# A two-layer graph network on one Trainium2 core: VectorE's instructions with two SBUF inputs cut into pieces of 128 columns

## The chip, the cores and the metric

The kernel runs on one NeuronCore of a Trainium2 chip, in a single launch. The metric is the device time of that launch in microseconds; the median of three runs counts. The engines are named as in the profile: PE is TensorE's matrix unit and PEld its weight loads, DVE is VectorE, ACT is ScalarE, POOL is GpSimd, SP is SyncE.

## The reference

There are 3,125 nodes of 128 features and 103,125 edges, sorted by destination, with 64 "radial" and 32 "spherical" features and one cutoff weight each. Cut to what matters:

```python
# layer 0: normalised graph convolution, residual, layer norm
norm = deg_inv_sqrt[src] * deg_inv_sqrt[dst]
h = x @ weight
out = segment_sum(norm[:, None] * h[src], dst)
x = layernorm(x + out + bias)
# layer 1: edge attention, residual, layer norm
w_ij = mlp(edge_64, rad_w0, rad_b0, rad_w1, rad_b1) + mlp(edge_32, sph_w0, sph_b0, sph_w1, sph_b1)  # hidden 256, silu
q, k, v = (x @ wq)[dst], (x @ wk)[src], (x @ wv)[src]          # 8 heads of 16
alpha = (q * w_ij * k).sum(per head) / sqrt(16) * cutoff
x = layernorm(x + segment_sum(alpha[..., None] * v, dst) / 16)
```

## The kernel before

Edges are padded to 202 groups of 512; a group is four tiles of 128 edges. An engine runs its own instruction list, and semaphores tie the lists together; the order on each engine is written out by hand.

**Sweep 1** (about 85 to 580 us of the span) has 51 unrolled steps. A step gathers seven tiles of source rows with indirect DMAs that POOL issues (line 794), sums them into a window of nodes by one-hot matmuls on PE (`sum1`, `add_tile`, line 1092), counts the rest of the edges with small one-hot products (lines 1475, 1476, 1492 on DVE), and runs the edge MLP for every fourth group, whose product goes to DRAM through `w_sb`. This product is the "stored" one.

**Sweep 2** (about 604 to 1665 us) has 51 steps of four groups: three unrolled, a loop of 11 turns with four steps in each, and four unrolled. For each group POOL gathers key and value rows eight groups ahead (`gather`, line 784, four indirect DMAs a group). PE expands the queries (`expand_q`, line 1218) and sums messages into the node window (`sum2`, line 1092). Of the four groups of a step, `g`, `g + 1`, `g + 2` and `g + 3`, the first takes its MLP product from DRAM through `w_sb` in SBUF; the other three have it computed on PE (`layer1`, lines 1066 and 1068; `layer2`, line 1084) and read it from PSUM.

On DVE a group passes through `times_k` (line 1670: key rows times queries), `times_w` (line 1682: times the MLP product), `head_sums` (line 1687), `times_cutoff` (line 1700) and `message` (line 1708: value rows times the attention factor). The factor of the stored group lies in `alpha` in SBUF, that of the others in PSUM. Around these stand `one_hot_t` (line 1661, the one-hot for `expand_q`), `one_hot` (line 1447, the one-hot for the sums), `add_pair` (line 1468) and `split_lo` (line 1454). MLP inputs are split into a rounded high half by ACT (line 892) and a low half by `split_lo`, 64 partitions by 1,024 columns in four instructions of 256; `layer1` reads both. One `split_lo` runs per sweep-1 step and three per sweep-2 step.

The order on DVE at the end of one step of sweep 2 and the head of the next is `one_hot_t(g + 6)`, `one_hot`, `times_k(g + 4)`, and then, with `g` now the next step's, `times_w(g - 1)`, `times_w(g)` from `w_sb`, `head_sums(g - 1)`, `split_lo`, `times_cutoff(g - 1)`, `times_k(g + 1)`, `message(g - 1)`, `head_sums(g)`, `one_hot_t(g + 3)`, `times_cutoff(g)`, `message(g)`. `one_hot_t(g + 6)` waits for PE's `expand_q(g + 4)`. On PE the list between those two points is the second half of one step and the first MLP group of the next:

```python
                expand_q(first + 4)
                expand_q(first + 5)
                sum2(first + 2)
...
                mlp_group(mlps[0], first + 1)
                expand_q(first + 2)
                if not s.before(1):
                    sum2(first - 1)
```

`sum2(first - 1)` waits for `message(g - 1)`.

Of the kernel before, what the change touches and what calls it, by code (L numbers as in the profile page):

```python
# [19 lines left out]
P = 128  # L20
WIN = 42
PARTS = 3
DIGITS = 64
TILES = 4
GE = P * TILES
HEADS, HD = 8, 16
RAD, SPH, HID = 64, 32, 256
# [18 lines left out]
F32 = mybir.dt.float32  # L46
# [3 lines left out]
ALU = mybir.AluOpType  # L50
# [83 lines left out]
def ds(start, size):  # L134
    return bass.DynSlice(start, size)


def build(nc, x, x_pad, src_idx, src_e, dst_e, dst_row, dst_first, cut_e, rad_t, sph_t, w_l0, b_l0, rad_w0, rad_b0,
          rad_w1, rad_b1, sph_w0, sph_b0, sph_w1, sph_b1, wq, wk, wv, out):
    N, D = x.shape  # L140
# [27 lines left out]
    with ExitStack() as ctx:  # L168
        def sb(name, shape, dt=F32):
            return ctx.enter_context(nc.sbuf_tensor(name, shape, dt))  # L170
# [6 lines left out]
        def sem(name):  # L177
            return ctx.enter_context(nc.semaphore(name))
# [21 lines left out]
        onehot = sb("onehot", [P, 2, 2 * TILES + 2, WIN])  # L200
        qwin = sb("qwin", [P, 2, D], BF16)
        xraw = sb("xraw", [RAD, 3, 2, GE])
        xsplit = sb("xsplit", [P, 2, 2, GE], F32R)
        hid = sb("hid", [P, 2, 4, GE])
        w_sb = sb("w_sb", [P, 2, TILES * D])
# [7 lines left out]
        rel = sb("rel", [P, COLS])  # L213
# [22 lines left out]
        iota_win = sb("iota_win", [P, WIN])  # L236
# [27 lines left out]
        def part(tile, at, n):  # L264

            return tile[:, at:at + n], at + n
# [7 lines left out]
        prod, to = part(late, 0, 2 * TILES * D)  # L274
        prod = prod.rearrange("p (k f) -> p k f", k=2)
        msg, to = part(late, to, 2 * TILES * D)
        msg = msg.rearrange("p (k t f) -> p k t f", k=2, t=TILES)
# [49 lines left out]
        w1_ps, w2_ps = bank[4:5], bank[3:5]  # L327
# [73 lines left out]
        mlp1, mlp2 = MlpSemaphores(sem, sems, 1, 2), MlpSemaphores(sem, sems, 2, 3)  # L401
# [6 lines left out]
        s_qkw = sem("s_qkw")  # L408
        s_red = sem("s_red")
        s_al = sem("s_al")  # L410
        s_msg = sem("s_msg")
# [874 lines left out]
        def _(dve):  # L1286
# [60 lines left out]
            for j in range(2):  # L1347
                own = slice(XS_DVE[j], XS_DVE[j + 1])
# [54 lines left out]
            for b in range(0, NB, 2):  # L1403
                own = slice(b, min(NB, b + 2))
                last = dve.tensor_tensor(xs_lo[:, own, :], xs_sb[:, own, :], xs_hi[:, own, :].bitcast(F32), ALU.subtract)
# [36 lines left out]
                dve.wait_ge(s_pass2, p * PASS2 + PASS2)  # L1442

            def one_hot(s, first=2 * TILES, n=2 * TILES):
                at = rel[:, ds(s.n * first, n)].unsqueeze(2).to_broadcast([P, n, WIN])
                nodes_in = iota_win[:, :].unsqueeze(1).to_broadcast([P, n, WIN])
                return dve.tensor_tensor(onehot[:, s.slot(2), 0:n, :], at, nodes_in, ALU.is_equal)

            def split_lo(s, mlp):
                dve.wait_ge(mlp.s_hi, s.tick + 1)  # L1450
                k, b = s.slot(mlp.ring), s.slot(2)
                for m in range(2):
                    for half in (slice(0, GE // 2), slice(GE // 2, GE)):
                        last = dve.tensor_tensor(xsplit[RAD:P, b, m, half], xraw[:, k, m, half],  # L1454
                                                 xsplit[0:RAD, b, m, half].bitcast(F32), ALU.subtract)
                last.then_inc(mlp.s_lo, 1)

            def load(row, first, n, most):
# [36 lines left out]
            def sweep1(s):  # L1495
                own = batches(s)
                if s.before(1):
                    one_hot(s, GATHERED, tiles1(s)).then_inc(s_hot1, 1)
                    split_lo(s, mlp1)
                    split_lo(s + 1, mlp1)  # L1500
                    for j in range(HOTS):
                        hots(own[0] + j)
# [15 lines left out]
                if product(s):  # L1518
                    span_bases = load(span_i, (product(s) * SPANS).n, SPANS, NP - 1)
                    if own:  # L1520
                        more_hots(own[0])
                        if not s.is_last(2):
                            split_lo(s + 2, mlp1)
                        dve.wait_ge(s_sum1, s.tick)
                        one_hot(s + 1, GATHERED, tiles1(s + 1)).then_inc(s_hot1, 1)
                    dve.wait_ge(s_acc1, s.tick)
                    add_spans(product(s), span_bases)
                    if own:
                        add_counts(own[0], offsets[0])
                        next_offset()  # L1530
                    batch(1)
                else:
                    batch(0)
                    batch(1)
                    if not s.is_last(2):
                        split_lo(s + 2, mlp1)
                batch(2)
                if not product(s):
                    if not s.before(1):
                        dve.wait_ge(s_sum1, s.tick)  # L1540
                    one_hot(s + 1, GATHERED, tiles1(s + 1)).then_inc(s_hot1, 1)
# [110 lines left out]
            def kv(g):  # L1652
                return gath2[:, g.slot(RING2), :].rearrange("p (t c f) -> p t c f", t=TILES, c=2)
# [19 lines left out]
            def times_w(g, s=None, m=None):  # L1673
                j = g.slot(2)
                dve.wait_ge(s_qk, g.tick + 1)
                if m is None:
                    dve.wait_ge(s_wload[s.slot(2)], (s.round(2) + 1) * 16)
                    w = w_sb[:, s.slot(2), :]
                else:
                    dve.wait_ge(mlp2.s_w, m.tick + 1)  # L1680
                    w = w2_ps[m.slot(2)][:, :]
                dve.tensor_tensor(prod[:, j, :], prod[:, j, :], w, ALU.mult).then_inc(s_qkw, 1)  # L1682

            def head_sums(g, turn=None):
                j = g.slot(2)
# [4 lines left out]
            def factors(m):  # L1690

                if m is None:
                    return alpha[:, :, :]
                return w2_ps[m.slot(2)][:, 0:TILES * HEADS].rearrange("p (t h) -> p t h", t=TILES)
# [7 lines left out]
            def message(g, m=None, turn=None):  # L1702
                j = g.slot(2)
                a = factors(m).unsqueeze(3).to_broadcast([P, TILES, HEADS, HD])
                dve.wait_ge(s_al, (turn or g).tick + 1)
                if not g.before(2):
                    dve.wait_ge(s_sum2, (g - 2).tick + 1)
                dve.tensor_tensor(msg[:, j, :, :].rearrange("p t (h d) -> p t h d", d=HD),  # L1708
                                  kv(g)[:, :, 1, :].rearrange("p t (h d) -> p t h d", d=HD), a,
                                  ALU.mult).then_inc(s_msg, 1)  # L1710
# [6 lines left out]
            def last_step2(s):  # L1717
                g, m, pairs = s.sub(4, 0, G), mlps2(s), pairs2(s)
                bases = load(base_i, s.n * 2 - 1, 2, NP - 1)
                times_w(g, s=s)  # L1720
                head_sums(g, turn=g - 1)
                times_cutoff(g, turn=g - 1)
                message(g, turn=g - 1)
                dve.wait_ge(s_relrow, s.p * 16 + 16)
                next_rows()
                times_w(g - 1, m=m[0] - 1)
                head_sums(g - 1, turn=g)
                times_cutoff(g - 1, m[0] - 1, turn=g)
                message(g - 1, m[0] - 1, turn=g)
                times_k(g + 1)  # L1730
                times_w(g + 1, m=m[0])
                head_sums(g + 1)
                times_cutoff(g + 1, m[0])
                message(g + 1, m[0])
                add_pair(pairs[0] - 1, bases[0])
                add_pair(pairs[0], bases[1])
# [81 lines left out]
class PRE:  # L1818
# [6 lines left out]
    half = 21  # L1825
# [3 lines left out]
class SET:  # L1829

    rel = 5
# [65 lines left out]
```

## Time and profile before

| | |
|---|---|
| time, median of 3 runs | 1691.49 us (1691.41 to 1692.15) |
| the profiled execution's own time | 1685.36 us |
| its span | 1683.5 us |
| PE busy | 1535.1 us (91%) |
| DVE busy | 1356.2 us (81%), 3810 instructions |
| POOL busy | 1215.7 us (72%) |
| ACT busy | 955.0 us (57%) |
| mean granted PE clock | 0.98 of full speed |

Busy time is the union of an engine's instructions. A row of the timeline gives start, length, line and shape; two DVE instructions can overlap, so the distance from one start to the next is what an instruction holds up its successor, and the length is what its reader waits for.

### The profile page before, as it was taken

The numbers are of one execution on the slowest core, as the hardware profiler recorded it, in microseconds if no ns is written. First come the engines' busy times: TensorE is split into PE (matmuls) and PEld (weight loads), VectorE is DVE, ScalarE is ACT, GpSimd is POOL, SyncE is SP. The second block draws the span as 40 slices with busy tenths as digits, with TensorE's granted clock in tenths as the row PEclk, the third lists the DMA queues.
The fourth block names the chain that finished last, engine by engine and source line by source line (L and its number), as shares of the span: only waits on it lengthen the run. The fifth ranks groups of instructions, "written<-read, shape, count | busy, mean of one in ns | idle before, by whom it ended". The sixth has DMA issues, their size and how long they took to land.

```text
span 1683.5 us, 43509 instructions
## 1 busy us (share of the span) xinstructions
PE 1535.1 (91%) x12636; PEld 1426.1 (85%) x12636; DVE 1356.2 (81%) x3810; ACT 955.0 (57%) x1410; POOL 1215.7 (72%) x1201
## 2 busy tenths in 40 slices
PE   4379999999999759999999999999999999999995
PEld 3267988888898749998989898989898989898995
DVE  9988779797887457887888787888787878887886
ACT  3344646566565465665656565655555656565664
POOL 5677777777777247777777777777777777777772
PEclk9999999999999889999999999999999999999998
DMA  4133334343433286666666666666666666666673
GB/s 123 39 97 108 109 102 116 108 121 103 116 108 97 64 231 170 189 190 172 186 183 184 174 186 173 185 182 180 180 180 180 184 178 185 181 186 179 183 190 115
DMA packets 176755, 257.32 MB, mean 153 GB/s; under 512 B 80278, under 2 KB 91213, under 8 KB 176476
## 3 DMA queue, kind: packets, MB, share of 16 engines
q0 software_dynamic: 50240, 129.44, 29.1%
q1 hardware_dynamic: 123100, 124.61, 25.0%
q10 hardware_dynamic: 3264, 1.64, 0.3%
q8 instruction: 48, 0.79, 0.2%
q14 instruction: 103, 0.84, 0.2%
HBM read 232.76 MB, written 22.79 MB: 152 GB/s over the span
## 4 chain that ended last, share of the span: by engine, by line
PE 66%; POOL 13%; issue 8%; DVE 7%; DMA 3%; ACT 1%; DVEq 1%; SPq 1%; POOLq 0%; ACTq 0%
PE bank L1084 33%; POOL arena L794 13%; PE bank L1092 12%; PE bank L1066 9%; PE bank L1068 4%; PE bank L1122 3%; PE bank L1218 3%; DVE arena L1323 2%; DMA arena<-xs_d,idx 1%; DMA idx<-in_src_e 1%; PE bank L1114 1%; DVE xsplit L1454 1%; DVE late L1670 1%; ACT nodes L948 0%; DVE red L1687 0%
## 5 line engine op out<-in xcount | busy, mean ns | idle before, releaser
L784 POOL DMA_INDIRECT arena<-kv_d,idx x808 | 802.5, 993 | 273.2 <-issue 259.8
L1084 PEld LDWEIGHTS bank<-w,hid 128*128 128x128 f32 x6464 | 781.9, 192 | 27.2 <-issue 1.9
L1084 PE MATMUL bank<-w,hid 128*128 128x128 f32 x6464 | 790.9, 276 | 0.0
L900 ACT ACTIVATE hid<-bank,b 128x512 f32<-128x512 f32 x808 | 500.6, 683 | 273.1 <-PE bank L1068 260.2
L794 POOL DMA_INDIRECT arena<-xs_d,idx x358 | 354.6, 991 | 128.8 <-issue 124.5
L1066 PE MATMUL bank<-xsplit,w_hi 128*128 128x512 f32 x808 | 347.7, 441 | 26.3 <-DVE xsplit L1454 26.3
L1454 DVE TENSOR_TENSOR xsplit<-xraw,xsplit 64x256 fp32r<-64x256 f32 x808 | 288.0, 414 | 7.3 <-ACT xsplit L892 1.0
L1092 PE MATMUL bank<-onehot,late 128*128 128x126 f32 x1616 | 219.2, 285 | 33.6 <-DVE late L1708 31.7
L1092 PEld LDWEIGHTS bank<-onehot,late 128*128 128x128 f32 x1616 | 196.7, 195 | 36.9 <-DVE late L1708 33.6
L892 ACT ACTIVATE xsplit<-xraw 64x1024 fp32r<-64x1024 f32 x202 | 210.7, 1044 | 2.6 <-DMA xraw<-in_sph_t 1.7
L884 ACT ACTIVATE bank<-b_full 128x512 f32<-128x512 f32 x199 | 119.3, 599 | 160.4 <-DVE late L1708 158.8
L1066 PEld LDWEIGHTS bank<-xsplit,w_hi 128*128 128x128 f32 x808 | 157.5, 195 | 50.1 <-DVE xsplit L1454 24.5
L1661 DVE TENSOR_SCALAR late<-late,iota_part 126x512 bf16<-126x512 bf16 x202 | 71.0, 352 | 115.5 <-PE bank L1218 113.9
L1068 PE MATMUL bank<-xsplit,w_lo 128*128 128x512 f32 x404 | 163.8, 405 | 0.0
L1492 DVE TENSOR_TENSOR count<-count,bank 128x300 f32 x225 | 103.9, 462 | 59.9 <-PE bank L1114 46.4
L1670 DVE TENSOR_TENSOR late<-arena,bank 128x512 f32<-128x512 f32 x202 | 137.8, 682 | 7.0 <-PE bank L1218 5.4
L1682 DVE TENSOR_TENSOR late<-late,bank 128x512 f32<-128x512 f32 x151 | 103.0, 682 | 47.8 <-issue 32.7
L1476 DVE TENSOR_SCALAR key_hot<-iota_key,key 128x300 bf16<-128x300 bf16 x450 | 140.9, 315 | 0.0
L1687 DVE TENSOR_REDUCE red<-late 128x32 f32<-128x512 f32 x202 | 137.1, 679 | 0.1
L919 ACT ACTIVATE w_sb<-bank 128x512 f32<-128x512 f32 x51 | 30.5, 598 | 163.3 <-PE bank L1084 163.3
L1475 DVE TENSOR_SCALAR low_hot<-iota_key,low_f 128x128 bf16<-128x128 bf16 x450 | 117.7, 262 | 3.2 <-issue 3.1
L1092 PE MATMUL bank<-onehot,arena 128*128 128x126 f32 x716 | 93.2, 278 | 17.3 <-DMA arena<-xs_d,idx 17.1
(159 smaller groups left out, 1358.6 us busy)
## 6 DMA issues: line engine op xcount, KB each, us to landing
xraw<-in_rad_t SPq DMA_DIRECT2D x207, 128.0 KB
xraw<-in_sph_t SPq DMA_DIRECT2D x414, 64.0 KB
late<-relrow_d SPq DMA_DIRECT2D x103, 256.0 KB, 3.9
w_sb<-w_d SPq DMA_DIRECT2D x52, 256.0 KB
w_d<-w_sb SPq DMA_DIRECT2D x51, 256.0 KB
arena<-kv_d,idx POOLq DMA_INDIRECT x808
arena<-xs_d,idx POOLq DMA_INDIRECT x358
qwin<-q_d SPq DMA_DIRECT2D x101, 31.5 KB
```

The lines of the kernel that those rows point to most:

```text
L784: pool.indirect_dma_start(gath[:, k, t * width:(t + 1) * width], None, table, bass.IndirectOffsetOnAxis(ap=idx[:, pair.slot(4), j * TILES ...
L794: pool.indirect_dma_start(gath1[s.slot(RING1)][:, t * D:(t + 1) * D], None, xs_d, bass.IndirectOffsetOnAxis(ap=idx[:, s.slot(4), t:t + 1], ...
L892: act.activation(xsplit[0:RAD, s.slot(2), :, :], xraw[:, k, :, :], ACT.Copy).then_inc(mlp.s_hi, 1)
L900: act.activation(hid[:, s.slot(2), c, :], hid_ps[s.sub(4, c, 4 * s.total).slot(len(hid_ps))][:, :], ACT.Silu, bias=b0[:, c:c + 1]).then_in ...
L1066: mm = pe.matmul(to, w0_hi[:, m, cols], xsplit[:, b, m, :], start=True, stop=(m == 1))
L1068: mm = pe.matmul(to, w0_lo[:, m, cols], xsplit[:, b, m, :], start=False, stop=True)
L1084: mm = pe.matmul(w_ps[:, t * D:(t + 1) * D], hid[:, b, c, t * P:(t + 1) * P], w1[:, c, :], start=False, stop=(c == 3), skip_group_check=True)
L1092: return pe.matmul(bank[7][:, 0:3 * WIN], rows, onehot[:, b, k:k + 3, :].rearrange("p t n -> p (t n)"), start=(k == 0), stop=(k == n - 1), ...
L1454: last = dve.tensor_tensor(xsplit[RAD:P, b, m, half], xraw[:, k, m, half], xsplit[0:RAD, b, m, half].bitcast(F32), ALU.subtract)
L1476: last = dve.tensor_scalar(key_hot[:, at_tile + t, :], iota_key[:, :], key[:, ds(col, 1)], None, ALU.is_equal)
L1670: dve.tensor_tensor(prod[:, j, :].rearrange("p (t f) -> p t f", t=TILES), kv(g)[:, :, 0, :], q_ps[j][:, :].rearrange("p (t f) -> p t f", t ...
L1687: dve.tensor_reduce(red[:, j, :, :].rearrange("p t h -> p (t h)"), prod[:, j, :].rearrange("p (h d) -> p h d", d=HD), AX.X, ALU.add).then_ ...
```

## The change

Four kinds of DVE instruction are cut along their columns; the data, the order and the waits stay, and the semaphore is raised by the last piece. `split_lo` has eight instructions of 128 columns for four of 256. `times_w` and `message` of the stored group have four of 128 for one of 512. `one_hot` has two of at most four tiles (168 columns each, or 168 and 126) for one.

```diff
             def one_hot(s, first=2 * TILES, n=2 * TILES):
-                at = rel[:, ds(s.n * first, n)].unsqueeze(2).to_broadcast([P, n, WIN])
-                nodes_in = iota_win[:, :].unsqueeze(1).to_broadcast([P, n, WIN])
-                return dve.tensor_tensor(onehot[:, s.slot(2), 0:n, :], at, nodes_in, ALU.is_equal)
+                for t in range(0, n, TILES):
+                    k = min(TILES, n - t)
+                    at = rel[:, ds(s.n * first + t, k)].unsqueeze(2).to_broadcast([P, k, WIN])
+                    nodes_in = iota_win[:, :].unsqueeze(1).to_broadcast([P, k, WIN])
+                    last = dve.tensor_tensor(onehot[:, s.slot(2), t:t + k, :], at, nodes_in, ALU.is_equal)
+                return last
...
                 for m in range(2):
-                    for half in (slice(0, GE // 2), slice(GE // 2, GE)):
-                        last = dve.tensor_tensor(xsplit[RAD:P, b, m, half], xraw[:, k, m, half],
-                                                 xsplit[0:RAD, b, m, half].bitcast(F32), ALU.subtract)
+                    for t in range(TILES):
+                        own = slice(t * P, (t + 1) * P)
+                        last = dve.tensor_tensor(xsplit[RAD:P, b, m, own], xraw[:, k, m, own],
+                                                 xsplit[0:RAD, b, m, own].bitcast(F32), ALU.subtract)
...
                 if m is None:
                     dve.wait_ge(s_wload[s.slot(2)], (s.round(2) + 1) * 16)
-                    w = w_sb[:, s.slot(2), :]
-                else:
-                    dve.wait_ge(mlp2.s_w, m.tick + 1)
-                    w = w2_ps[m.slot(2)][:, :]
-                dve.tensor_tensor(prod[:, j, :], prod[:, j, :], w, ALU.mult).then_inc(s_qkw, 1)
+                    for t in range(TILES):
+                        own = slice(t * D, (t + 1) * D)
+                        last = dve.tensor_tensor(prod[:, j, own], prod[:, j, own], w_sb[:, s.slot(2), own], ALU.mult)
+                    last.then_inc(s_qkw, 1)
+                    return
+                dve.wait_ge(mlp2.s_w, m.tick + 1)
+                dve.tensor_tensor(prod[:, j, :], prod[:, j, :], w2_ps[m.slot(2)][:, :], ALU.mult).then_inc(s_qkw, 1)
...
+                if m is None:
+                    for t in range(TILES):
+                        last = dve.tensor_tensor(msg[:, j, t, :].rearrange("p (h d) -> p h d", d=HD),
+                                                 kv(g)[:, t, 1, :].rearrange("p (h d) -> p h d", d=HD), a[:, t, :, :], ALU.mult)
+                    last.then_inc(s_msg, 1)
+                    return
```

## Rows read from the trace of the kernel before

**Rows 1.** Busy time by stretch: stretch, length, engines, granted clock, DMA share, GB/s.

```profile
900.00:1100.00 200.00, 193.13 (x1561) 184.08 (x1560) 164.95 (x389) 117.74 (x175) 153.33 (x154) 0.97 0.66 180
```

**Rows 2.** PE's waits, whole run: who waited for whom, us in total, times, longest.

```profile
PE bank L1092 <- DVE late L1708: 31.7, 11, 3.7
PE bank L1066 <- DVE xsplit L1454: 26.3, 3, 14.8
PE bank L1092 <- DMA arena<-xs_d,idx: 17.1, 16, 1.8
```

**Rows 3.** DVE's waits from 700 to 1500 us, a stretch of sweep 2.

```profile
DVE late L1661 <- PE bank L1218: 90.1, 39, 2.4
DVE late L1682 <- issue: 29.2, 9, 3.9
```

**Rows 4.** PE's timeline: start, length, instructions; in brackets the idle time before.

```profile
307.61 0.93 PE L1092 MATMUL bank<-onehot,arena 128*128 128x126 f32 x6 [1.15 <-DMA arena<-xs_d,idx]
...
861.65 1.16 PE L1092 MATMUL bank<-onehot,late 128*128 128x126 f32 x8 [2.86 <-DVE late L1708]
...
1028.29 2.08 PE L1092 MATMUL bank<-onehot,late 128*128 128x126 f32 x8 [3.57 <-DVE late L1708]
...
1081.91 0.61 PE L1218 MATMUL bank<-qwin,late 126*128 126x128 bf16 x8
...
1088.27 0.39 PE L1218 MATMUL bank<-qwin,late 126*128 126x128 bf16 x4
1088.49 1.11 PE L1092 MATMUL bank<-onehot,late 128*128 128x126 f32 x8
```

**Rows 5.** DVE's timeline, at a loop turn and in three later steps of sweep 2.

```profile
1027.55 0.68 DVE L1708 TENSOR_TENSOR late<-arena,bank 128x512 f32<-128x512 f32 x1
...
1057.84 0.20 DVE L1700 TENSOR_TENSOR bank<-red,cut 128x32 f32<-128x32 f32 x1
1057.94 0.35 DVE L1661 TENSOR_SCALAR late<-late,iota_part 126x512 bf16<-126x512 bf16 x1
...
1064.69 0.69 DVE L1682 TENSOR_TENSOR late<-late,w_sb 128x512 f32<-128x512 f32 x1
...
1082.33 0.35 DVE L1661 TENSOR_SCALAR late<-late,iota_part 126x512 bf16<-126x512 bf16 x1 [2.30 <-PE bank L1218]
1082.60 0.50 DVE L1447 TENSOR_TENSOR onehot<-rel,iota_win 128x336 f32<-128x336 f32 x1
1083.02 0.68 DVE L1670 TENSOR_TENSOR late<-arena,bank 128x512 f32<-128x512 f32 x1
1083.62 0.68 DVE L1682 TENSOR_TENSOR late<-late,bank 128x512 f32<-128x512 f32 x1
...
1085.53 1.43 DVE L1454 TENSOR_TENSOR xsplit<-xraw,xsplit 64x256 fp32r<-64x256 f32 x4
...
1087.70 0.68 DVE L1708 TENSOR_TENSOR late<-arena,bank 128x512 f32<-128x512 f32 x1
```

**Rows 6.** `split_lo` as a group by line and shape: busy us, mean ns, idle before.

```profile
L1454 DVE TENSOR_TENSOR xsplit<-xraw,xsplit 64x256 fp32r<-64x256 f32 x808 | 288.0, 414 | 7.3 <-ACT xsplit L892 1.0
```

**Rows 7.** Line 1670, `times_k`, whole run: its lengths, then its only idle time before.

```profile
L1670 DVE TENSOR_TENSOR late<-arena,bank x202: 677/681/689, 624.8 to 1660.0; 128x512 f32<-128x512 f32 x101
...
  PE bank L1218: 5.4, 1
```

**Rows 8.** POOL's timeline in sweep 2, three gathers in a row.

```profile
1064.89 1.31 POOL L784 DMA_INDIRECT arena<-kv_d,idx  x1 [0.30 <-issue]
1066.51 1.08 POOL L784 DMA_INDIRECT arena<-kv_d,idx  x1 [0.31 <-issue]
1067.89 0.94 POOL L784 DMA_INDIRECT arena<-kv_d,idx  x1 [0.30 <-issue]
```

**Rows 9.** The gathers as groups by line: busy us, mean ns, idle before.

```profile
L784 POOL DMA_INDIRECT arena<-kv_d,idx x808 | 802.5, 993 | 273.2 <-issue 259.8 <-DVE late L1708 13.4
...
L794 POOL DMA_INDIRECT arena<-xs_d,idx x358 | 354.6, 991 | 128.8 <-issue 124.5 <-DMA idx<-in_src_e 3.7 <-PE bank L1092 0.6
```

## The prediction

> **What bounds the kernel now.** I read the busy times by stretch first. In sweep 2 PE is busy for 193.13 of 200 us, DVE for 164.95 [rows 1]: PE sets the pace there, and DVE looks as if it had room. A mean cannot say where that room lies, so I went on to the waits. From 700 to 1500 us DVE waits 39 times, 2.3 us each, before `one_hot_t(g + 6)` for PE's `expand_q`, once in each step [rows 3]. PE itself waits for `message` before `sum2` 11 times in the run, 31.7 us together [rows 2]. Ten of these follow a stall of DVE's own, about 3 us of "issue" when its loop jumps back [rows 3].
>
> The timelines of one ordinary step then show how much room there is. PE starts its pair of `expand_q` at 1081.91; DVE, waiting for it, starts `one_hot_t` at 1082.33 [rows 4, 5]. From there DVE runs without a pause through `one_hot`, `times_k`, both `times_w`, `head_sums`, `split_lo`, `times_cutoff`, `times_k` to `message(g - 1)`, which ends at 1087.70 + 0.68 = 1088.38. PE wants it at 1088.49, right behind the `expand_q` that began at 1088.27 [rows 4, 5]. At the turn, where PE does stand waiting, it starts 0.06 us after the message ends (1027.55 + 0.68 = 1028.23, then 1028.29). So the ordinary step has a cover of 0.11 - 0.06 = 0.05 us. DVE's 2.3 idle microseconds stand ahead of this chain, which PE itself starts; they cannot be spent inside it. That is the place to price the change: whatever lengthens the stretch from `one_hot_t` to `message(g - 1)` by more than 0.05 us lengthens the step, because PE is full for the rest of it.
>
> **What a piece costs.** An instruction holds up the next by the distance between starts: 0.10 us for 32 columns (1057.84 to 1057.94), 0.60 for 512 (1083.02 to 1083.62) [rows 5]; for 256 it is (1.43 - 0.414) / 3 = 0.339 [rows 5, 6]. The line from 32 to 256 columns has 1.067 ns a column and 0.066 us fixed. A piece of 128 columns thus holds 0.203, one of 168 0.245.
>
> - `split_lo`: 8 x 0.203 for 4 x 0.339: 1.62 for 1.36, +0.26.
> - `times_w` of the stored group: 4 x 0.203 for 0.60: +0.21. `message` of the stored group: the same.
> - `one_hot`: 2 x 0.245 for 0.42 (1082.60 to 1083.02 [rows 5]): +0.07.
>
> The lower bound for eight more instructions in the chain is nothing, if pieces overlapped wholly, but even 32 columns hold 0.10. The line through 256 and 512 columns gives 0.078 fixed and 0.62 for the chain. The upper bound is that pieces don't overlap at all: a length of 0.414 - 128 x 0.001067 = 0.277 each gives 2.22 for 1.36, 1.11 for 0.60 and, with 0.50 - 0.18 = 0.32, 0.64 for 0.42, or +1.6 us. I take 0.066, since the pieces are of the kind that the 1.43 us row already shows overlapping.
>
> By the Trainium skill ("VectorE: DVE Perf Modes", section "The DRAIN you can't avoid") the next instruction cannot issue until the pipe is empty, and instruction count is what to keep down. By that the sum would be near the upper bound; the rows, four of 0.414 in 1.43, do not show so long a gap.
>
> **The chain, step by step.** It holds one `one_hot`, the stored `times_w` and one `split_lo`: 0.07 + 0.21 + 0.26 = +0.54 us. `message` of the stored group and the other two `split_lo` come behind `message(g - 1)`; they take 0.21 + 0.07 + 2 x 0.26 = 0.8 us from DVE's wait. That wait goes from 2.3 to 2.3 + 0.5 (PE is later by so much) - 0.54 - 0.8, or about 1.4 us, so it still covers them. If that cover went, the whole 1.4 us a step would show.
>
> Of 51 steps 49 have this `sum2` (the first has no earlier group, the last is written apart). Ten follow a jump back of the loop and wait already: 10 x 0.54 = 5.4. The other 39 have 0.05 of cover: 39 x 0.49 = 19.1. Together +24.5 us.
>
> **The clock at the turns.** After an idle 3.57 us eight matmuls took 2.08 us, after 2.86 us 1.16, after none 1.11 [rows 4]. A longer idle at the turns can put some of the undisturbed ones on the lower level; two more at about 1 to 1.5 us are +2.5, between 0 and 8. The 0.5 us idle of an ordinary step should not do it: six matmuls behind 1.15 us of idle took 0.93 [rows 4].
>
> **Ends.** Each pass begins with a `split_lo` for which PE stands waiting [rows 2], and DVE's last step has a stored `message` on its path: about +1.
>
> **Sweep 1 and POOL.** Here something can be won. Line 794's gathers take 0.991 us in the mean [rows 9], while an undisturbed gather takes 0.94 [rows 8]. The long ones fall on the edited instructions: the gather at 1064.89 took 1.31 and began while `times_w` from `w_sb` ran (1064.69 to 1065.38) [rows 5, 8]. So a gather waits for the end of a DVE instruction with two SBUF inputs, and shorter pieces let it in sooner. In sweep 1 this lengthening is 358 x 0.05 = 18 us at most; `split_lo` and `one_hot` are only part of it, and halving them leaves some 5. PE waits 17.1 us there for gathers [rows 2], so it can use that; but `split_lo` and `one_hot` add 0.33 us to each of 51 steps on DVE. From -10 (more of the lengthening goes) to +17 (all of DVE's addition shows); I take -3, because PE waits for gathers in this sweep and not for DVE.
>
> **Sum.** 24.5 + 2.5 + 1 - 3 = +25 us against the profiled execution's 1685.36 (span 1683.5 and 1.9 around it): 1710. The median of the runs lies 6.1 us above that execution, which gives 1716.
>
> **Rivals.**
>
> *Gathers set the pace, and it gets faster.* POOL issues gathers through all of sweep 2 with 0.3 us between them [rows 8], 808 of 0.993 us [rows 9]. If their landing ended last, the change would give back about half of 808 x 0.05 = 40 us of lengthening, and 5 in sweep 1: -25, or 1666. It decides only from the point where `times_k` waits for a gather. Against it: no `times_k` waited for one; its only wait in the run is 5.4 us, once, for PE [rows 7]. Chance 0.07.
>
> The Trainium skill ("SBUF — State Buffer", section "SBUF: two separate sides") has the rule behind this: a port pair shared by VectorE and GpSimd is locked for the whole instruction, also by one with two SBUF inputs. The long gathers agree; what that does for the time hangs on who waits for them.
>
> *DVE's room hides it, and nothing changes.* 1.4 us more a step fit into 2.3 of idle; with -3 and +1 the time would be 1690. For it stands the mean load [rows 1], against it the order: 0.05 us of cover in the chain. Chance 0.07.
>
> *Pieces cost their whole length, or the clock falls in ordinary steps.* +1.6 in the chain would be 49 x 1.55 = 76 us, 1767; half of that, or some 20 to 30 steps with a falling clock at 1 us, 1735 to 1745. Against it are the overlapping four of `split_lo` and the 1.15 us idle above. Chance 0.08.
>
> **How the numbers follow.** The forecast has 0.78, with 1703 to 1732 as its own range: 0.62 instead of 0.54 in the chain (+4), the clock (-2.5 to +5.5), sweep 1 (-7 to +20, both ends unlikely). The range 1698 to 1732 leaves out the faster rival, nearly all of the one that hides it and most of the dear one, together just under 0.2. A change of 0.2% (3.4 us) is about what measurement here can tell from none. Faster has the first rival's 0.07, same the second's 0.07, slower 0.86.
>
> **What would show it.** Right: in the changed kernel's timeline PE is idle about half a microsecond before `sum2` in every ordinary step, ended by `message`; the waits' view has some 50 of these for 11 before, some 55 us together; DVE's wait before `one_hot_t` is near 1.4 us; eight `split_lo` pieces take about 1.7 us from first start to last end; gathers are shorter in the mean, near 0.97; an ordinary step of sweep 2 is half a microsecond longer. Wrong: DVE's wait is unchanged and PE's waits stay at 11 (the cover held), `times_k` waits for DMA (gathers paced it), pieces 0.28 us apart, or sweep 1 longer by 10 us.

## The result and the profile after

The changed kernel takes 1715.24 us in the median of 4 runs (1714.82 to 1715.6); the kernel before takes 1691.45 (1690.0 to 1692.15). The ratio is 1.0142, 95% interval 1.0126 to 1.0158: slower by 1.4%, 0.8 us from the forecast of 1716. The profiled execution took 1715.35 us, its span 1713.5.

Busy time from 900 to 1100 us, against [rows 1]:

```profile
900.00:1100.00 200.00, 189.74 (x1533) 179.54 (x1532) 175.62 (x568) 113.66 (x170) 145.77 (x152) 0.98 0.62 178
```

DVE has 568 instructions for 389 and is busy 10.7 us more; PE, which set the pace, is busy 3.4 us less. PE's waits in the whole run, against [rows 2]:

```profile
PE bank L1092 <- DVE late L1720: 50.8, 50, 3.9
...
PE bank L1066 <- DVE xsplit L1458: 27.0, 3, 15.2
PE bank L1092 <- DMA arena<-xs_d,idx: 13.1, 13, 1.9
```

Fifty waits for `message` (line 1720 now) where there were 11. DVE's waits from 700 to 1500 us, against [rows 3]:

```profile
DVE late L1665 <- PE bank L1218: 51.4, 37, 1.9
DVE late L1688 <- issue: 29.5, 9, 3.4
```

Before `one_hot_t` DVE waits 1.39 us for 2.31; the stall of "issue" at the jump back is as long as it was. The timelines of an ordinary step and of a turn, PE first, against [rows 4, 5]:

```profile
1097.52 0.39 PE L1218 MATMUL bank<-qwin,late 126*128 126x128 bf16 x4
1098.23 1.16 PE L1092 MATMUL bank<-onehot,late 128*128 128x126 f32 x8 [0.32 <-DVE late L1720]
...
1117.59 0.39 PE L1218 MATMUL bank<-qwin,late 126*128 126x128 bf16 x4
1121.63 1.57 PE L1092 MATMUL bank<-onehot,late 128*128 128x126 f32 x8 [3.65 <-DVE late L1720]
```

```profile
1091.59 0.35 DVE L1665 TENSOR_SCALAR late<-late,iota_part 126x512 bf16<-126x512 bf16 x1 [1.25 <-PE bank L1218]
1091.86 0.57 DVE L1449 TENSOR_TENSOR onehot<-rel,iota_win 128x168 f32<-128x168 f32 x2
...
1093.54 0.89 DVE L1684 TENSOR_TENSOR late<-late,w_sb 128x128 f32<-128x128 f32 x4
...
1095.05 1.70 DVE L1458 TENSOR_TENSOR xsplit<-xraw,xsplit 64x128 fp32r<-64x128 f32 x8
...
1097.50 0.68 DVE L1720 TENSOR_TENSOR late<-arena,bank 128x512 f32<-128x512 f32 x1
...
1116.33 0.69 DVE L1688 TENSOR_TENSOR late<-late,bank 128x512 f32<-128x512 f32 x1 [3.23 <-issue]
```

`message` ends at 1097.50 + 0.68 = 1098.18 and PE starts 0.05 us later. From the start of the last `expand_q` to `sum2` it is 0.71 us; in the step of [rows 4] it was 0.22 (1088.27 to 1088.49). So this step has 0.49 us more. Over the 39 ordinary steps that distance went from 0.25 to 0.72 us in the mean, and an ordinary step of the loop, from one such `sum2` to the next, from 19.59 to 20.08 us. (The bracket has only 0.32, since the `expand_q`'s own end is modelled later than its successor could have started.) The gathers, against [rows 9], came down:

```profile
L784 POOL DMA_INDIRECT arena<-kv_d,idx x808 | 779.7, 965 | 311.4 <-issue 262.8 <-DVE late L1720 48.6
L794 POOL DMA_INDIRECT arena<-xs_d,idx x358 | 350.7, 980 | 128.8 <-issue 126.4 <-DMA idx<-in_src_e 1.5 <-PE bank L1092 0.9
```

**Where the time went.** The two profiled executions differ by 30.0 us. The first gather of sweep 2 starts 1.3 us earlier (604.47 to 603.17), and from there to the first `sum2` that waits for `message(g - 1)` it is 0.2 us more; from that `sum2` to the 49th of its kind, one a step, it is 1013.86 us for 984.45 (+29.4); behind that +1.7. The +29.4 splits by steps. At each of ten turns, the step of the stall and the one after it take 45.17 us for 43.58, +1.59: 15.9. The other 28 steps have 0.48 each: 13.5.

### The profile page after: what moved, and what is told of

It reads as the page before. It is cut to its first block, busy times and chain, and to the rows that moved or that the text cites. A ratio compares the mean times of both kernels' runs of the same rounds, so it can differ in the third digit from the quotient of the medians.

```text
span 1713.5 us, 44863 instructions
## 1 busy us (share of the span) xinstructions
PE 1549.1 (90%) x12636; PEld 1433.0 (84%) x12636; DVE 1453.2 (85%) x5076; ACT 954.9 (56%) x1410; POOL 1190.2 (69%) x1201
## 4 chain that ended last, share of the span: by engine, by line
PE 49%; DVE 19%; POOL 14%; issue 11%; DVEq 3%; DMA 2%; ACT 1%; SPq 0%; POOLq 0%; ACTq 0%
PE bank L1084 24%; POOL arena L794 14%; PE bank L1092 10%; PE bank L1066 6%; DVE xsplit L1458 4%; PE bank L1068 3%; DVE late L1684 3%; DVE late L1674 2%; DVE arena L1323 2%; PE bank L1122 2%; DVE late L1720 2%; DVE red L1693 2%; DVEq L1464 1%; PE bank L1218 1%; PE bank L1114 1%
## 5 line engine op out<-in xcount | busy, mean ns | idle before, releaser
L784 POOL DMA_INDIRECT arena<-kv_d,idx x808 | 779.7, 965 | 311.4 <-issue 262.8
L794 POOL DMA_INDIRECT arena<-xs_d,idx x358 | 350.7, 980 | 128.8 <-issue 126.4
L1066 PE MATMUL bank<-xsplit,w_hi 128*128 128x512 f32 x808 | 351.9, 446 | 27.0 <-DVE xsplit L1458 27.0
L1458 DVE TENSOR_TENSOR xsplit<-xraw,xsplit 64x128 fp32r<-64x128 f32 x1616 | 346.3, 280 | 6.4
L1066 PEld LDWEIGHTS bank<-xsplit,w_hi 128*128 128x128 f32 x808 | 159.4, 197 | 51.5 <-DVE xsplit L1458 24.9
L1665 DVE TENSOR_SCALAR late<-late,iota_part 126x512 bf16<-126x512 bf16 x202 | 77.1, 382 | 70.8 <-PE bank L1218 66.3
L1092 PE MATMUL bank<-onehot,arena 128*128 128x126 f32 x716 | 92.2, 277 | 13.3 <-DMA arena<-xs_d,idx 13.1
```

Of the source, the lines that this page charges most:

```text
L784: pool.indirect_dma_start(gath[:, k, t * width:(t + 1) * width], None, table, bass.IndirectOffsetOnAxis(ap=idx[:, pair.slot(4), j * TILES ...
L794: pool.indirect_dma_start(gath1[s.slot(RING1)][:, t * D:(t + 1) * D], None, xs_d, bass.IndirectOffsetOnAxis(ap=idx[:, s.slot(4), t:t + 1], ...
L1066: mm = pe.matmul(to, w0_hi[:, m, cols], xsplit[:, b, m, :], start=True, stop=(m == 1))
L1092: return pe.matmul(bank[7][:, 0:3 * WIN], rows, onehot[:, b, k:k + 3, :].rearrange("p t n -> p (t n)"), start=(k == 0), stop=(k == n - 1), ...
L1458: last = dve.tensor_tensor(xsplit[RAD:P, b, m, own], xraw[:, k, m, own], xsplit[0:RAD, b, m, own].bitcast(F32), ALU.subtract)
```

## The experiments

Theory A is the prediction's reason: the cuts on the chain from `one_hot_t` to `message(g - 1)` cost 0.49 us a step, those behind it are covered. Its first rival now is that the other cuts, or the gathers, carry the difference. Line numbers of the experiments are up to a dozen off from those above.

**Only the chain's cuts** (against the kernel before, with the stored `times_w` in four as in the change):

```diff
-                split_lo(m[2], mlp2)
+                split_lo(m[2], mlp2, 128)
...
-                one_hot(pairs[1] + 1)
+                one_hot(pairs[1] + 1, cut_up=True)
```

> Only the three instructions of sweep 2 that stand in the chain from one_hot_t(g + 6) to message(g - 1) are cut: the stored times_w, the split_lo before times_cutoff, the one_hot ahead of times_k(g + 4). All else is as before. Theory A (the chain has 0.05 us of cover, so what is in it shows and what is behind it does not): nearly the whole loss, 1713 to 1719, PE idle about 0.49 us before sum2 in each ordinary step. Theory B (VectorE's added load shows, wherever it stands): 0.54 of 1.35 us per step, so some 10 us, 1701. Theory C (shorter pieces matter through GpSimd's gathers): GpSimd's mean gather in sweep 2 falls by what the times_w and a third of the split_lo collisions cost, and the time falls below 1690.

Measured: 1750.44 us (1749.19 to 1754.61), ratio 1.0372 [1.0352, 1.0392]. The ordinary step is 20.07 us (one in four 20.37), with the 0.49 us before `sum2` that theory A wants, but the total is 35 us too long. DVE's timeline at a turn shows why:

```profile
1043.17 0.69 DVE L1690 TENSOR_TENSOR late<-late,bank 128x512 f32<-128x512 f32 x1 [3.82 <-issue]
1046.17 0.90 DVE L1686 TENSOR_TENSOR late<-late,w_sb 128x128 f32<-128x128 f32 x4 [2.32 <-issue]
```

At each turn there are two stalls of "issue", 3.8 and 2.0 us in the mean of ten, where the kernel before and the changed kernel have one. Nothing in the second instruction's inputs is late: its load from DRAM was issued 25 us ahead of it (1020.59), and loads of this kind land in some 4 us. This was not in any theory.

**Only the cuts behind the chain** (stored `message` in four, the other two `split_lo` in eight, the other one-hot in two; cut to the lines on `split_lo`, against the kernel just above):

```diff
-                size = size or (256 if mlp is mlp1 else 256)
+                size = size or (256 if mlp is mlp1 else 128)
...
-                split_lo(m[2], mlp2, 128)
+                split_lo(m[2], mlp2, 256)
```

> The opposite half of sweep 2: only the stored message, the two split_lo behind message(g - 1) and the one_hot behind it are cut, 0.8 us more VectorE time per step. Theory A: PE's waits stay at about 11 and the time within 3 us of before, 1688 to 1695; VectorE's wait before one_hot_t falls from 2.3 to about 1.5 us. Theory B: 0.8 of 1.35 us per step, so some 14 us, 1705. Theory C: below 1690.

Measured: 1672.77 us (1669.3 to 1674.08), ratio 0.9905 [0.9888, 0.9922]: faster than both kernels, and by its time alone theory C's. The ordinary step is 19.6 us at first, so these cuts are covered (from the 18th step on steps are longer, for the reason found in the next section). But the stalls at the turns are gone, and with them half of the traffic of the queue that loads instructions (packets, MB, share), the kernel before first:

```profile
q14 instruction: 103, 0.84, 0.2%
```

```profile
q14 instruction: 54, 0.44, 0.1%
```

So the turn's stall looks like a wait for instructions, whose absence may have won the time in theory C's place. The Trainium skill ("Runtime: NRT & Kernel Launch", section "Instruction fetch mechanics") says that an engine holds two blocks of 256 instructions, and that a taken branch whose target is in neither forces a fetch. The fall of that queue's packets with the stalls agrees. I call it theory P: the stall hangs on where the loop of sweep 2 lies, and each experiment moves it.

**Only sweep 1's cuts** (cut to two of the lines, against the kernel just above):

```diff
-                size = size or (256 if mlp is mlp1 else 128)
+                size = size or (128 if mlp is mlp1 else 256)
...
-                    one_hot(s, GATHERED, tiles1(s), False).then_inc(s_hot1, 1)
+                    one_hot(s, GATHERED, tiles1(s), True).then_inc(s_hot1, 1)
```

> Only sweep 1's split_lo and one_hot are cut. Prediction's term: -3 us, from GpSimd being let in sooner (bounds -10 and +17). From the two traces I expect -1 to -3 us: 1688 to 1691, with the mean gather of line 794 at about 0.980 us for 0.991 and PE's waits for these gathers at about 13 us for 17. If VectorE's addition of 0.33 us a step shows instead: up to 1708.

Measured: 1689.29 us (1681.96 to 1693.49), ratio 0.9991 [0.9972, 1.001], between a gain of 4.7 us and a loss of 1.7. Line 794's gathers went from 991 to 978 ns.

**All cuts, the message of the group before moved ahead of `split_lo` and the stored `times_w`** (against the changed kernel):

```diff
-                times_w(g, s=s)
                 if not s.before(1):
                     head_sums(g - 1)
-                split_lo(m[2], mlp2)
-                if not s.before(1):
                     times_cutoff(g - 1, m[0] - 1)
-                times_k(g + 1)
-                if not s.before(1):
                     message(g - 1, m[0] - 1)
+                split_lo(m[2], mlp2, 128)
+                times_w(g, s=s)
+                times_k(g + 1)
```

> All cuts of the change stay, but in sweep 2 head_sums, times_cutoff and message of group g - 1 come right behind its times_w, ahead of split_lo, the stored times_w and times_k(g + 1). VectorE has the same work in another order. Theory A: the chain to message(g - 1) loses about 3.0 us of other work and gains some 0.3 us of latency between dependent instructions, so PE waits for no message in ordinary steps and about 1 us instead of 4 at the ten turns of the loop: 24 us of the change's loss and another 20 to 35 us at the turns come back, 1655 to 1672. Theory B: the same load, so 1715 or somewhat more for the latencies.

Measured: 1686.46 us (1683.93 to 1690.25), ratio 0.9989 [0.9976, 1.0001]. Most of the loss is gone, but 1655 to 1672 is missed. PE's waits:

```profile
PE bank L1066 <- DVE xsplit L1460: 40.8, 27, 15.2
...
PE bank L1092 <- DVE late L1722: 14.3, 19, 1.6
```

The ordinary step is back to 19.6 us with nothing ahead of `sum2`; near the turns `split_lo`, now behind the message, is late in its place, and DVE's stall there is unchanged (29.9 us in nine from 700 to 1500).

### Moving the loop

The next kernels have one-element memsets put ahead of sweep 2's loop, in idle time of DVE, which changes nothing in the loop but its place:

```diff
+                    if s.is_last(1):
+                        for k in range(39):
+                            dve.memset(unused[0:1, k:k + 1], 0.0)
                     dve.wait_ge(s_acc1, s.tick)
                     add_spans(product(s), span_bases)
```

**The kernel before, moved by 39.**

> The kernel before with 39 one-element memsets of VectorE put into its idle time at the end of sweep 1, so that the loop of sweep 2 stands 39 instructions later; the work of the loop is untouched. Theory P (the 3.3 us in which VectorE waits for nothing the profile shows, once at each of 9 to 10 turns of the loop, come from where the loop's instructions stand, not from what they do): these waits fall from 29 us to under 3. Then either the whole turn is won back (two steps of 43.6 us at a turn against 39.1 for two ordinary ones, 10 times: 1645 to 1650 us), or GpSimd's gathers, issued without a pause from 604 to 1652 us in the kernel before, become the bound and the time is 1678 to 1688 us; I take the second. Theory W (the waits belong to the turn itself): waits as before, 1689 to 1693 us.

Measured: 1680.41 us (1678.0 to 1685.25), ratio 0.9941 [0.9918, 0.9964]. No stall is left at any turn, and the instruction queue has 53 packets: theory P holds, theory W falls. Of the 32.7 us of stalls 11 came back, between the medians. The profiled execution is the slowest of the eight (1685.25 us), so its rows show what took the rest at its largest. PE now waits elsewhere, for `hid` 31 times in the run:

```profile
PE bank L1067 <- ACT hid L901: 27.8, 31, 1.7
...
PE bank L1093 <- DVE late L1720: 3.6, 11, 0.4
```

Steps are 19.55 us for the first thirteen (20.1 at the turns), then 19.8 to 21.8. In the POOL timeline 64 gathers (four steps) start 82.3 to 83.6 us apart here and 82.6 to 83.8 in the kernel before, whose turns are 82.9 us apart: there PE with its stall and the gathers kept the same pace by chance. Without the stall PE runs ahead until a group's last gather ends only 4 to 7 us before its `times_k` (11 to 18 in the loop of the kernel before), and from there the gathers are the bound. How they hold PE back is in two waits from 1300 to 1500 us, of SP's queue and of ACT, and in the chain of waits of that stretch:

```profile
SPq L522 <- DMA arena<-kv_d,idx: 83.5, 19, 5.2
```

```profile
ACT xsplit L893 <- DMA xraw<-in_sph_t: 23.1, 18, 2.6
```

```profile
by line: POOL arena L785 75.8%; issue 22.3%; POOLq L805 1.7%; POOLq L783 0.3%; POOLq L801 0.3%; POOLq L122 0.1%
```

Line 522 is SP's `load_idx`: it may reuse an index buffer only when the gathers that read it have landed. Behind it in SP's queue stand the loads of `xraw`; these come late, ACT's `split_hi` waits for them, `hid` is late, and PE with it. `times_k` waits for a gather once in the run, for 0.4 us.

**The chain's cuts alone, moved by 107.**

> The chain's cuts alone, as in the first experiment, with 107 memsets that move the loop so that its start is not at the end of a block of 256 instructions. Theory A (the chain from one_hot_t to the message costs 0.5 us a step, and the 35 us that the first experiment showed beyond the changed kernel came from a second wait for instructions at each turn): only one wait of about 3.3 us at a turn, ordinary step 20.05 us, 1712 to 1720 us, as the changed kernel. Rival (the chain's cuts really cost 60 us alone, and the other cuts give 35 back): 1745 to 1755 us again.

Measured: 1720.46 us (1718.41 to 1721.49), ratio 1.017 [1.0133, 1.0206]. One stall at a turn, ordinary step 20.08 us. PE's waits for `message` in the whole run, and DVE's stalls from 700 to 1500 us:

```profile
PE bank L1093 <- DVE late L1720: 52.4, 50, 4.2
```

```profile
DVE late L1694 <- issue: 31.4, 9, 3.8
```

There are fifty waits for `message`, as in the changed kernel: the chain's cuts alone make the loss of the whole change. Of the 30 us that the first experiment took above this, 29 lie in the pairs of steps at its ten turns. The second stall itself is 20 of them; the rest, with a longer first stall (3.8 us for 3.5), was not taken apart.

**The cuts behind the chain, moved by 76.**

> The cuts behind the chain alone (stored message, the two other split_lo, the other one-hot), as in the second experiment, with 76 memsets that move the loop to where one wait at each turn is to be expected again. Theory A (these cuts are covered by VectorE's idle time, and the 19 us won in the second experiment were the turn's wait): waits of 3 us at each turn are back, ordinary step 19.55 us, 1687 to 1694 us. Rival (the cuts themselves win time by keeping GpSimd's gathers short): 1670 to 1676 us again.

Measured: 1692.21 us (1687.17 to 1695.31), ratio 0.9998 [0.9979, 1.0017]. The stalls are back (31.4 us in ten), the ordinary step is 19.55 us. PE's waits for `message` in the whole run, and DVE's waits from 700 to 1500 us:

```profile
PE bank L1093 <- DVE late L1726: 30.8, 11, 3.3
```

```profile
DVE late L1671 <- PE bank L1219: 54.2, 37, 2.2
DVE late L1694 <- issue: 28.2, 9, 3.4
```

PE waits 11 times, as in the kernel before, and DVE's wait before `one_hot_t` falls to 1.46 us: it is what covers them. These cuts cost nothing that can be measured (-3.6 to +2.9 us), and the 19 us won in the second experiment were the stall's.

**The stored weight product in eight pieces of 64** (all other cuts as in the change):

```diff
-                    for t in range(TILES):
-                        own = slice(t * D, (t + 1) * D)
+                    for t in range(0, GE, 64):
+                        own = slice(t, t + 64)
```

> The changed kernel with the stored weight product in eight pieces of 64 columns instead of four of 128; its loop turns with one wait, as the changed kernel's. Theory A (each piece costs its fixed 0.066 us, all of it on the chain): four more pieces are 0.26 us a step, the wait of TensorE before sum2 grows from 0.49 to 0.75 us, 49 steps: 1715 + 13, that is 1726 to 1731 us. Rival (a shorter piece costs its full length anew, as the third rival of the prediction had it): step longer by over 0.5 us, 1740 us or more. Rival (slack is left): 1715 to 1718 us.

Measured: 1736.0 us (1733.14 to 1737.31), ratio 1.026 [1.0223, 1.0297]. DVE's eight pieces, and PE's last `expand_q` and `sum2`, in one step:

```profile
1062.59 1.17 DVE L1686 TENSOR_TENSOR late<-late,w_sb 128x64 f32<-128x64 f32 x8
...
1066.57 0.39 PE L1218 MATMUL bank<-qwin,late 126*128 126x128 bf16 x4
1067.56 1.16 PE L1092 MATMUL bank<-onehot,late 128*128 128x126 f32 x8 [0.60 <-DVE late L1722]
```

From start to start it is 0.99 us, 0.77 over the 0.22: four more pieces cost 0.28 us, 0.07 each, against 0.066 expected. The total is 5 us above the range: one step in four has 0.2 us more, which I did not follow up, and at all ten turns PE's eight matmuls took 1.79 to 2.08 us, for 1.37 to 1.68 in the changed kernel.

**The changed kernel with the chain's `split_lo` in four, moved by 28.**

```diff
-                split_lo(m[2], mlp2, 128)
+                split_lo(m[2], mlp2, 256)
```

> The changed kernel, but the split_lo on the chain in four instructions as before, with 28 memsets that keep the end of the loop where it stands in the changed kernel. Theory A (each instruction of the chain costs its fixed 0.066 us, TensorE's wait before sum2 is their sum less 0.05): four fewer are 0.26 us, the wait falls from 0.49 to 0.23 us, 49 steps: 1715 - 13, that is 1700 to 1705 us. Rival (split_lo is covered by its neighbours, the stored product alone holds the message back): 1713 to 1717 us.

Measured: 1706.3 us (1705.88 to 1709.8), ratio 1.0094 [1.0058, 1.013], 1 us above the range. Its step:

```profile
1090.20 0.39 PE L1219 MATMUL bank<-qwin,late 126*128 126x128 bf16 x4
1090.64 1.16 PE L1093 MATMUL bank<-onehot,late 128*128 128x126 f32 x8
```

0.44 - 0.22 = 0.22 us, where theory A says 0.23; ordinary step 19.80 us. So `split_lo` is 0.27 of the 0.49, the stored product and the one-hot the rest. The two steps of a turn take 45.09 us, nearly the 45.17 of the changed kernel although the chain is shorter by 0.54 in them: at seven of the ten the eight matmuls took 2.07 us, against 1.68 at most in the changed kernel. That accounts for the 4 us by which the gain of 13 fell short: 10 x (0.54 - 0.08) = 4.6.

**The changed kernel, moved by 225.**

> The changed kernel with 225 memsets ahead of sweep 2's loop (130 in the idle time at the end of sweep 1, 95 before the nodes' product), which put the start of the loop just behind the start of a block of 256 instructions and its end in the first half of the next but one. Theory P: no wait of VectorE for instructions at the turns, no fall of the clock there, ordinary steps of 20.07 us throughout, since the gathers are 14 us or more ahead; 10 turns of 45.2 us become 40.1: 1715 - 50, that is 1662 to 1672 us. The chain's cuts still cost their 0.49 us a step. Rival (GpSimd binds first, as in the kernel before moved): steps grow beyond 20.07 us and the time is 1675 to 1685 us. Rival W (no effect of the place): 1712 to 1718 us.

Measured: 1716.21 us (1713.06 to 1716.89), ratio 1.014 [1.0104, 1.0177]. The stalls stayed (33.7 us in ten), and so did the time, in rival W's range. Since 39 instructions did remove them from the kernel before, the place does count, but theory P as I had it was incomplete: a loop that starts behind a block's start can still be too long.

**The early message with all cuts, moved by 225.**

> All cuts, the message of the group before moved ahead of split_lo, the weight product and times_k (as in the fourth experiment), and the loop moved by 225 memsets as in the run beside it. If the fourth experiment missed its 1655 to 1672 us through the waits at the turns, they are gone here: ordinary step 19.6 us at first, then GpSimd's gathers bind, at a mean of 0.963 us against 0.99 in the kernel before moved (808 of them, 22 us less than its 1680): 1655 to 1668 us. Rival (the early message makes split_lo late in every step): ordinary step over 20 us, 1670 us or more.

Measured: 1688.13 us (1683.58 to 1693.67), ratio 0.9981 [0.9965, 0.9998]. The stalls stayed here too (36.1 us in ten), the time is that of the fourth experiment, and the 1655 to 1668 are missed with it.

**The early message, all `split_lo` and the stored `times_w` cut, one-hots and stored message whole, moved by 34** (cut to two of the lines, against the kernel above):

```diff
-                one_hot(pairs[1] + 1, cut_up=True)
+                one_hot(pairs[1] + 1, cut_up=False)
...
-                        for k in range(130):
+                        for k in range(34):
```

> All three split_lo and the stored weight product cut, the one-hots and the stored message whole, the message of the group before moved ahead of the chain (as in the fourth experiment), and 34 memsets; the loop is 329 instructions long, starts just behind the start of a block of 256 and ends 76 into the next but one, two instructions short of where the second experiment's loop ended, which had no wait at its turns (the changed kernel moved, 30 further on, had it at each). Theory: no wait at the turns; the cuts are off the path of sum2, so ordinary steps are 19.55 us; gathers of sweep 2 at a mean of 0.965 to 0.972 us against 0.990 in the kernel before moved (808 of them, 15 to 20 us off its 1680), so 1658 to 1668 us. Rival (the loop is too long and waits at each turn after all): 1682 to 1690 us, as the two runs with the early message. Rival (gathers stay at 0.98 us and bind): 1669 to 1676 us.

Measured: 1672.12 us (1668.6 to 1678.09), ratio 0.989 [0.9865, 0.9916], by the second rival's range. There is no stall at any turn, and the first steps take 19.55 us with nothing before `sum2`, although `split_lo` and `times_w` are cut: the same pieces off the chain are free. From the 18th step on the gathers bind again, in the same way (from 1300 to 1500 us SP's `load_idx` waits 85.5 us for them), at a mean of 0.980 us:

```profile
L785 POOL DMA_INDIRECT arena<-kv_d,idx x808 | 791.5, 980 | 271.9 <-issue 267.7 <-DVE late L1720 4.3
```

With the second experiment it is the fastest here, 1.1% below the kernel before and 2.5% below the changed one.

### What the places say together

Places are counted from the program's order, modulo the 256 instructions that a block has by the Trainium skill ("Runtime: NRT & Kernel Launch", section "Instruction fetch mechanics"), plus 24. The 24 is an estimate: it puts the block's end between the two instructions of the first experiment that stall one after the other. All these loops reach into a second block; the first experiment's reaches into a third.

| kernel | instructions in loop | starts at | ends at | stalls at a turn |
|---|---|---|---|---|
| before, moved by 39 | 269 | 8 | 20 | none |
| early message, moved by 34 | 329 | 4 | 76 | none |
| cuts behind the chain | 321 | 14 | 78 | none |
| changed, moved by 225 | 357 | 6 | 106 | one, 3.4 us |
| changed | 357 | 37 | 137 | one, 3.3 us |
| chain moved by 107 | 305 | 100 | 148 | one, 3.5 us |
| before | 269 | 225 | 237 | one, 3.3 us |
| chain only | 305 | 249 | 41 | two, 3.8 and 2.0 us |

No stall is seen when the loop starts just behind a block's start and ends within 78 instructions of the next. The kernels left out here stall once at each turn and fit: sweep 1's cuts alone lie at 224 to 236, the eight pieces at 49 to 165, `split_lo` in four at 53 to 137, the cuts behind the chain moved by 76 at 90 to 154, and the two with all cuts and the early message where the changed kernel and the changed one moved by 225 lie. (The expectations of the kernels moved by 225 and by 34 put the end into the next block but one; by this count it is the next.) Why an end at 106 is too far when the start lies in the block just before it, the runs don't show.

## Why the prediction was right, and where it was mis-sized

- **The chain** was right in kind and size. Predicted: 0.54 us in DVE's chain, 0.05 of cover, 24.5 us. Measured: 0.48 in the ordinary step and, at each of ten turns, 1.11 in two steps (from the last `expand_q` to `sum2` 4.13 and 0.74 us, for 3.53 and 0.23, in the mean): 28 x 0.48 + 10 x 1.11 = 24.5 us. The cover was read from one step; it is the usual one, but in the kernel before every fourth step had none, with 0.30 to 0.33 us from the last `expand_q` to `sum2` where the others have 0.22. The chain alone makes the loss (moved by 107: 1720.46), the rest alone none (moved by 76: 1692.21), four instructions less take 0.27, four more add 0.28, and moved off the path to `sum2` they cost nothing.
- **The price of a piece** was right: eight `split_lo` in 1.70 us, four of `times_w` in 0.89; by the forecast's figures 7 x 0.203 + 0.277 = 1.70 and 3 x 0.203 + 0.277 = 0.89. The rival that pieces cost their whole length falls with the dose: 0.07 us for one more. The section of the Trainium skill weighed there ("VectorE: DVE Perf Modes", "The DRAIN you can't avoid") has the next operation wait until the pipe is empty, but also says that one which is not held starts earlier; the forecast weighed only the first. The pieces did start earlier: one of 64 columns held up the next by (1.17 - 0.219) / 7 = 0.14 us, at a mean length of 0.219.
- **The clock at the turns** was the term that was mis-sized: +2.5 was forecast between the profiled executions; what is left of the turns is 15.9 - 11.1 = 4.8, and PE has no other wait over 0.1 us in those steps. The granted clock fell to 0.50 of full speed, the lower of the two levels (1.2 GHz), at six of ten turns in the kernel before and at all ten in the changed one. In the kernel before the eight matmuls after the stall took 1.7 to 2.08 us at those six (granted clock 0.50 from 1028.29 to 1030.40 us) and 1.16 at four; in the changed kernel they took 1.37 to 1.68 at all ten, and the matmuls behind them are slow too (0.77 us for 0.48 for the first `L1066` after the turn above). Executions of one kernel differ in it: two runs of the kernel before took 1685.08 us at a mean granted clock of 0.981 and 1698.21 at 0.97.
- **From the profiled execution to the median** the forecast added 6.1 us for both kernels. The changed kernel's profiled execution lies at its median (1715.35 and 1715.24), so between the profiles the forecast was 5 us short (25 for 30.0), and between the medians 1 over (25 for 23.8). I put both down to the clock at the turns: a usual execution of the kernel before pays for it what its profiled one did not. This is argued and not shown, since a median has no trace. Two things speak for it. Over the 70 executions of the kernel before on record, a granted clock 0.01 lower goes with some 11 us more (an estimate, the line through their times and clocks). The run with sweep 1's cuts alone, whose sweep 2 is that of before, is the other: its profiled execution took 1689.16 us, and its turn pairs 44.29 us for 43.58, 7 us in ten. So between medians the clock is worth about 4.8 - 6.1 = -1.3, and with the chain's 24.5, -1.3 ahead of sweep 2 and 0.2 + 1.7 at its ends it is 23.8. That the forecast came within 0.8 us is luck: two errors, of one cause by this account, cancel.
- **Sweep 1, the ends and POOL**: -1.3 us for -3, and +1.9 at the ends for about +1; sweep 1's cuts alone are between -4.7 and +1.7. The gathers fell to 0.965 us in sweep 2, as forecast, where nothing waited for them. In sweep 1 PE's waits for them fell by 4.0 us (17.1 to 13.1), of which 1.3 arrived; what took the rest I did not follow.
- **The rivals.** That gathers set the pace was given 0.07 because no `times_k` waits for one. For this change that came out right, but the point at which it decides was misplaced: gathers bind through SP's `load_idx` and the `xraw` loads behind it, while `times_k` still finds its data. In the changed kernel's loop a group's last gather ends 19 to 28 us before its `times_k`, so they are further from binding than before. That DVE's room hides the change is wrong by place: the cuts behind the chain are hidden, those in it are not.
- **What the prediction took for granted** without saying so: that the stall at the turn stays as it is when 88 instructions are added to the loop. It did, 3.3 us for 3.3, but by chance of place: of these kernels three lost it and one got a second.

## What to carry to other kernels

Price a cut by where each instruction stands between two hand-overs of the bounding engine, not by the engine's mean load: the same pieces cost 0.5 us a step ahead of `message` and nothing behind it. After any edit that adds instructions to a loop, look for "issue" waits at its jump back before reading the edit's own effect: here moving the loop alone was worth 11 to 30 us (1691 to 1680, 1692 for 1673, 1750 to 1720), as much as the change. When a stall is taken away, ask what else keeps the same pace; here the gathers let only 11 us of 33 come back.

## What was not expected of the hardware

- A loop's jump back cost VectorE 3.0 to 3.9 us of "issue" wait, each turn, in the kernel before, whose loop is 269 instructions long, and nothing after 39 instructions were put ahead of it; in one place a second wait of 2.0 us came behind the first.
- The long gathers of [rows 8] are those behind VectorE instructions with two SBUF inputs: in sweep 2 of the kernel before, all 82 gathers over 1.1 us began while one ran, in the changed kernel 18 of 19. With the four kinds cut, sweep 2's mean fell from 993 to 965 ns, as the port rule of the Trainium skill ("SBUF — State Buffer", section "SBUF: two separate sides") would have it; with those of the last experiment, to 980. But the mean does not hang on the cuts alone: with the chain's cuts it was 978 ns at the loop's first place and 997 after the move by 107. What sets it there was not followed.
- Where `sum2` started 3.0 to 3.1 us late, PE's eight matmuls took 1.16 us at some turns and 2.07 at others of one execution (kernel before); 3.7 to 4.0 us late in the changed kernel, 1.37 to 1.68. Why the same wait ends at two clocks stays open.
